# A decoder with a delta-rule layer: the inverses of its diagonal blocks in groups of four units, not eight

## The reference

```
q, k, v = silu(conv(x @ Wq)), silu(conv(x @ Wk)), silu(conv(x @ Wv))   # HK = 16 heads, q and k of 128, v of 256
q, k = l2norm(q), l2norm(k)
alpha, beta = sigmoid(x @ Wa), sigmoid(x @ Wb)
def step(state, (qt, kt, vt, at, bt)):
    state = state * at
    err = vt - einsum('bhkv,bhk->bhv', state, kt)
    state = state + bt * einsum('bhk,bhv->bhkv', kt, err)
    return state, einsum('bhkv,bhk->bhv', state, qt)
x = x + outs @ Wo
```

## Time and profile before

| what | value |
|---|---|
| median of 3 runs | 4774.38 us (4768.8 to 4774.94) |
| profiled execution | 4788.41 us, span 4786.6 us |
| busy in the span: PE, DVE, ACT, POOL | 82%, 58%, 34%, 28% |
| the delta layer | about 1518 to 3260 us |
| there: PE, DVE, ACT, POOL busy | 1645.6, 1354.4, 823.6, 889.1 us |
| mean granted clock of TensorE | 0.918 |

### The profile page before, as it was taken

How to read it: one execution, slowest core, us unless ns; L and a number is a source line. 1 busy time by engine, 2 the same in 40 slices (tenths; PEclk the granted TensorE clock), 3 DMA queues, 4 the chain that set the end, 5 groups by cost and what they waited for, 6 DMA issues and landing times. The chain is left out here.

```text
span 4786.6 us, 58979 instructions
## 1 busy us (share of the span) xinstructions
PE 3923.9 (82%) x18543; PEld 2940.0 (61%) x18543; DVE 2799.6 (58%) x7765; ACT 1611.4 (34%) x3960; POOL 1349.6 (28%) x2074
## 2 busy tenths in 40 slices
PE   6999976999997799999999999983999999960230
PEld 4666654555555578888888888872556565640230
DVE  4666654222222788888888888844666666653123
ACT  2444431111111455545455554521444444420000
POOL 0000000000000365455555455540111111116447
PEclk9999986999997999999999999996999999985665
DMA  1000000000000011111111111111000000011240
GB/s 65 0 0 0 0 8 24 12 12 23 12 12 18 20 37 23 41 38 24 36 23 40 35 29 36 24 18 51 1 0 0 0 0 0 0 64 58 60 143 13
DMA packets 198749, 119.39 MB, mean 25 GB/s; under 512 B 122312, under 2 KB 187654, under 8 KB 197520
## 3 DMA queue, kind: packets, MB, share of 16 engines
q1 hardware_dynamic: 181472, 102.85, 8.3%
q0 software_dynamic: 12288, 9.55, 0.7%
q10 hardware_dynamic: 4800, 4.72, 0.3%
HBM read 102.09 MB, written 38.93 MB: 29 GB/s over the span
## 5 line engine op out<-in xcount | busy, mean ns | idle before, releaser
L1630 DVE SCALAR_TENSOR_TENSOR dl_y<-ps,dl_taps,dl_y 128x255 f32<-128x255 f32 (+2 forms) x1536 | 653.0, 474 | 131.4 <-ACT dl_y L1526 127.3
L1361 PE MATMUL ps<-xnT,dl_wkqv 128*128 128x256 f32 x2048 | 543.4, 391 | 33.9 <-DVE dl_lp L1673 26.4
L923 PE MATMUL ps<-xnT,moe_wgu 128*112 x1024 | 447.3, 595 | 5.2 <-DVE moe_ex L963 5.2
L1361 PEld LDWEIGHTS ps<-xnT,dl_wkqv 128*128 128x128 f32 x2048 | 367.9, 193 | 84.0 <-issue 39.2
L923 PEld LDWEIGHTS ps<-xnT,moe_wgu 128*112 128x112 f32 x1024 | 181.9, 178 | 251.3 <-issue 249.3
L362 POOL TENSOR_TENSOR at_rs<-at_ss,mhalf 128x15 f32<-128x15 f32 x32 | 125.5, 3921 | 745.9 <-DVE at_ss L549 745.9
L183 POOL TENSOR_TENSOR ln_rstd<-ln_ve,mhalf 128x4 f32<-128x4 f32 x24 | 24.2, 1010 | 1084.0 <-DVE ln_ve L169 1084.0
L1284 POOL TENSOR_TENSOR dl_rn<-dl_n,mhalf 128x4 f32<-128x4 f32 x128 | 173.7, 1357 | 548.2 <-DVE dl_n L1646 548.2
L448 PE MATMUL ps<-at_shared,at_v 128*128 128x256 f32 (+2 forms) x1280 | 315.9, 380 | 4.6
L989 DVE TENSOR_TENSOR moe_hT<-moe_sg,ps 112x1024 f32<-112x1024 f32 x64 | 78.2, 1221 | 372.6 <-ACT moe_sg L947 372.6
L1526 ACT ACTIVATE dl_y<-ps,dl_taps 128x256 f32<-128x256 f32 x512 | 260.2, 560 | 95.4 <-PE ps L1361 95.4
(11 more groups left out here) (278 smaller groups left out, 8195.3 us busy)
## 6 DMA issues: line engine op xcount, KB each, us to landing
dl_grow<-decay_rows SPq DMA_DIRECT2D x128, 128.0 KB, 3.0
sp_wgu<-in_w1gu SPq DMA_DIRECT2D x12, 768.0 KB, 10.2
dl_wkqv<-in_w1kqv SPq DMA_DIRECT2D x16, 512.0 KB, 4.7
delta_diag<-dl_lp SPq DMA_DIRECT2D x512, 8.0 KB, 1.5
dl_diag<-delta_diag_tt SPq DMA_DIRECT2D x512, 8.0 KB, 1.7
moe_wgu<-in_w0gu SPq DMA_DIRECT2D x16, 448.0 KB, 3.7
slot_rows<-sp_zero SPq DMA_DIRECT2D x4, 1152.0 KB, 8.1
sp_wd<-in_w1d SPq DMA_DIRECT2D x12, 384.0 KB, 11.5
```

The lines of the kernel that those rows point to most:

```text
L923: last = nc.tensor.matmul(k.ps[h][0:IC, m, :], wgu[q][h][:, c, m * IC:(m + 1) * IC], k.xnT[:, c, ds(g * (GT * P), GT * P)], start=c == 0, ...
L1361: last = nc.tensor.matmul(bank(h, m // 2, (m % 2) * S, (m % 2 + 1) * S), wkqv[h][:, c, m * P:(m + 1) * P], k.xnT[:, c, u.seq * S:(u.seq + ...
L1630: last = nc.vector.scalar_tensor_tensor(y[h][:, m, back:S], bank(h, m // 2, (m % 2) * S, (m % 2 + 1) * S - back), taps[h][:, m, KC - 1 - b ...
```

## The change

Groups are of four units (GI = 4) on 32 partitions, and each is inverted in four stages, all four of which have two parts: `CUTS` has eight. LAG is 2 * GI + 2 = 10. `inv_a` has two buffers, so that its load waits for the end of the inversion before the last. A group is now named by the unit's number alone. On SP, `load_a` stands directly behind the last dump of its group, and `store_inverse` at the first grown unit of its group.

```diff
@@ -1020,16 +1020,19 @@
...
 
+GI = 4
+
+
 class Group:
...
 
-    def __init__(self, j, g):
-        self.j, self.g = j, g
-        self.parity = g % 2
-        self.real = not isinstance(j, int) or 0 <= 2 * j + g < HK * B // 8
+    def __init__(self, n):
+        self.g, self.inst = n // GI, n % GI
+        self.parity = self.g % 2
+        self.real = 0 <= n < HK * B
 
     def count(self, per, more=0):
-        return self.j * (2 * per) + (self.g * per + more)
+        return self.g * per + more
 
...
@@ -1078,15 +1081,13 @@
...
     Q32 = 32
-    GI = 8
     GP = GI * 8
...
     STEPS = 2 + 2 * (Q32 - 2)
-    CUTS = (1, 4, 6, 9, 11, 14, 16, 18, 20, 23, 25, 28, Q32 - 1)
-    CHUNKS = 6
-    LAG = 16
+    CUTS = (1, 5, 9, 13, 17, 20, 24, 28, Q32 - 1)
+    LAG = 2 * GI + 2
     scratch = nc.dram_tensor("decay_rows", (HK, T), F32, kind="Internal").ap()
...
@@ -1122,7 +1123,7 @@
...
 
-        inv_a = sb("inv_a", [GP, Q32, Q32])
+        inv_a = [sb(f"inv_a{i}", [GP, Q32, Q32]) for i in range(2)]
         inv_flat = sb("inv_u", [GP, Q32 * (Q32 + 1)])
...
@@ -1184,18 +1185,18 @@
...
 
-                def dump_diag(u, g, inst):
+                def dump_diag(u, g):
 
...
                         r = slice(b * Q32, (b + 1) * Q32)
-                        sp.dma_start(ldump[g.parity, o, inst].rearrange("b r c -> r b c"),
+                        sp.dma_start(ldump[g.parity, o, g.inst].rearrange("b r c -> r b c"),
                                      lp[u.h][r, u.seq, 0:2 * S].rearrange("p (b s) -> p b s", b=2)[:, :, r]).then_inc(dumped, 16)
...
                     sp.wait_ge(dumped, g.count(GI * 4 * 16, GI * 4 * 16))
-                    wait_past(sp, inv_done, g.count(1))
-                    sp.dma_start(inv_a[:, :, :], ldump[g.parity].rearrange("o i b r c -> (o i b) r c")).then_inc(a_loaded, 16)
+                    wait_past(sp, inv_done, g.count(1, -1))
+                    sp.dma_start(inv_a[g.parity][:, :, :], ldump[g.parity].rearrange("o i b r c -> (o i b) r c")).then_inc(a_loaded, 16)
 
...
@@ -1203,28 +1204,24 @@
...
 
-                def load_diag(u, g, inst):
+                def load_diag(u, g):
 
...
                         r = slice(b * Q32, (b + 1) * Q32)
-                        sp.dma_start(diag[u.h][r, :, r], ttdump[g.parity, o, inst].rearrange("b r c -> r b c"))\
+                        sp.dma_start(diag[u.h][r, :, r], ttdump[g.parity, o, g.inst].rearrange("b r c -> r b c"))\
                             .then_inc(diag_loaded[u.h], 16)
...
                         sp.dma_start(diag_t[u.h][o * HALF:o * HALF + Q32, :, o * Q32:(o + 1) * Q32],
-                                     tdump[g.parity, o, inst].rearrange("b r c -> r b c")).then_inc(diag_loaded[u.h], 16)
+                                     tdump[g.parity, o, g.inst].rearrange("b r c -> r b c")).then_inc(diag_loaded[u.h], 16)
 
                 def stage(j, s, project, prepared, turned, grown, given):
-                    first = Group(j, (s - 9) // 8)
-                    if s % 8 == 1 and first.real:
-                        load_a(first)
-                    if s % 8 == 7:
-                        done = Group(j, (s - 15) // 8)
-                        if done.real:
-                            store_inverse(done)
-                    ready = Unit(j, s - 15)
+                    n = 2 * B * j + s
+                    ready = Group(n - (LAG - 1))
                     if ready.real:
-                        load_diag(ready, Group(j, (s - 15) // 8), (s - 15) % 8)
+                        if ready.inst == 0:
+                            store_inverse(ready)
+                        load_diag(Unit(j, s - (LAG - 1)), ready)
                     ahead = Unit(j, s + 1)
...
@@ -1235,7 +1232,10 @@
...
                     if prepared is not None:
-                        dump_diag(prepared, Group(j, (s - 1) // 8), (s - 1) % 8)
+                        full = Group(n - 1)
+                        dump_diag(prepared, full)
+                        if full.inst == GI - 1:
+                            load_a(full)
 
...
@@ -1286,7 +1286,7 @@
...
                     wait_past(pool, inv_stored, g.count(32))
-                    nc.gpsimd.tensor_tensor(inv_u, inv_a[:, :, :], inv_mask[:, :, :], ALU.mult).then_inc(inv_step, 1)
+                    nc.gpsimd.tensor_tensor(inv_u, inv_a[g.parity][:, :, :], inv_mask[:, :, :], ALU.mult).then_inc(inv_step, 1)
                     pool.wait_ge(inv_step, g.count(STEPS, 1))
...
@@ -1297,7 +1297,7 @@
...
                     nc.gpsimd.tensor_tensor(tmp, inv_u[:, 0:i, i:i + 1].to_broadcast([GP, i, w]),
-                                            inv_a[:, i:i + 1, i + 1:Q32].to_broadcast([GP, i, w]), ALU.mult).then_inc(inv_step, 1)
+                                            inv_a[g.parity][:, i:i + 1, i + 1:Q32].to_broadcast([GP, i, w]), ALU.mult).then_inc(inv_step, 1)
                     pool.wait_ge(inv_step, g.count(STEPS, 2 * i + 1))
...
@@ -1312,20 +1312,20 @@
...
                         eliminate(g, i)
-                    if part == 2 * CHUNKS - 1:
+                    if part == 2 * GI - 1:
                         end_inverse(g)
...
                 def stage(j, s, project, prepared, turned, grown, given):
-                    g, part = Group(j, (s - 9) // 8), (s - 1) % 8
-                    inverting = g.real and part < CHUNKS
+                    g = Group(2 * B * j + s - GI - 1)
+                    inverting = g.real
                     if prepared is not None:
...
                     if inverting:
-                        invert_part(g, 2 * part)
+                        invert_part(g, 2 * g.inst)
                     if prepared is not None:
...
                     if inverting:
-                        invert_part(g, 2 * part + 1)
+                        invert_part(g, 2 * g.inst + 1)
 
...
@@ -1418,7 +1418,7 @@
...
 
-                    pe.wait_ge(v_scaled[h], min(u.count(1, B), B * HK // 2) if u.fixed else u.count(1, B))
+                    pe.wait_ge(v_scaled[h], min(u.count(1, LAG // 2), B * HK // 2))
                     for blk in range(2):
...
@@ -2212,7 +2212,7 @@
...
     r, q = np.arange(32)[:, None], np.arange(32)[None, :]
-    c["c_invmask"] = np.broadcast_to(np.where(q > r, -1.0, 0.0).astype(np.float32), (64, 32, 32))
+    c["c_invmask"] = np.broadcast_to(np.where(q > r, -1.0, 0.0).astype(np.float32), (32, 32, 32))
     return c
...
```

## The result

The changed kernel takes 4833.31 us (median of 4 runs, 4826.41 to 4840.09) where the kernel before took 4774.66 in as many runs beside it: a ratio of 1.0122, 95% interval 1.0100 to 1.0144, so 58.7 us slower. The forecast was 4861 (+87), with a range of 4795 to 4920. Its direction and its mechanism held; it was too high by 28 us. In the experiments further down one run of e3 stood apart, with 5242 us where its other five took 4750 to 4755; the ratio is of those five.

The account below looks back on a forecast made before the run. PE with DVE paced the kernel before; POOL would bound the changed one. First to last pow +111.8 us, drain -25.2, together +86.6: profiled 4788.41 becomes 4875.0, less 14.0 to the median, 4861 us, range 4795 to 4920.

Parts of the forecast that it names:

- The drain: The layer's end after the last pow: 25.2 us less, 24.0 of it from fewer units behind the last inversion.
- POOL's instructions cost the same on 32 partitions: POOL's inversion on 32 partitions takes the same 38.91 us per group as on 64, run 32 times instead of 16.
- The rival "faster": POOL's operations cost half on 32 partitions; late gap 13.0 us, total about 4724 us; chance 0.06.
- The three gaps without a load: The three intervals between pows in a group that hold no load: 35.71 us of POOL work plus 1.8 of stalls.
- The pow: POOL's power of each unit's lengths (L1284), starting each stage: hardly waits for DVE, 1.02 us rather than 1.40.
- The first gap: Interval between pows at a group's start: 10.1 us until load and stores land, 5.72 for the first part, 15.8 together.
- The sum: First to last pow: 30.3 us of fill plus 31 groups of 53.3 give 1682.6, +111.8; with the drain +86.6.
- POOL becomes the bound, by 2 us a group: POOL paces the stages: 53.3 us per group of four, where the other engines could do it in 51.4.
- The waits: DVE waits 150 us or more for the pow; POOL about 90% busy, PE 93%; 32 L1289 waits of about 4 us.
- What was costed at nothing: Second inv_a, head weights, load_diag behind the stores, and PE's clock in the fill: each taken to add no time.
- The gentle case: Everything hides but the load, no stalls: 50.7 us a group, 4780 us (4776 to 4825); chance 0.18.
- the heavy case: Load and stores in series (12.24 us), or full lock between POOL and DVE: 4926 to 4932 us; chance 0.08 (above 4915).

Follow-up runs that it names:

- e3: Changed kernel with two buffers for inv_u, each group's inversion begun one stage later and LAG 12: 0.9953 of the kernel before, 4751.23 us.
- e5: Changed kernel with DVE's first L1640 of a stage reading its second operand from PSUM: 1.0053 of the kernel before.
- e11: Changed kernel with 11 eliminations left out of the middle of each group's inversion, first and last part whole: 1.0008 of the kernel before.
- e8: Changed kernel, LAG 10 kept, with the pow ahead of the inversion's start in a group's first stage: 1.0007 of the kernel before.
- e10: Changed kernel, LAG 10, with the pow first, two buffers for inv_u and two POOL copies per stage removed: 0.9952 of the kernel before.
- e6: Kernel before (groups of eight, LAG 16) with each of a group's 60 eliminating instructions issued twice: 1.0376 of the kernel before.
- e9: Kernel before (groups of eight, LAG 16) with the pow ahead of the inversion in a group's first stage: 0.9968 of the kernel before.
- e7: e3 with POOL relieved of two copies per stage, ACT using three activations instead of two: 0.9877 of the kernel before.
- e4: Changed kernel with 13 of each group's 30 eliminations left out, the wait kept: 1.0082 of the kernel before.

## Why the prediction was right, and where its sizes were off

**The drain.** Forecast: 25.2 us less. From the last pow to the end of the last add it was 116.0 us and is 3322.88 + 0.88 - 3233.53 = 90.2: 25.8 less. Right, though divided a little differently: behind the last inversion it is 25.2 less and not 24.0, while its start comes 12.55 us after the pow, hardly sooner than the 12.7 of before, where 10 to 12 was forecast.

```profile
L1284 POOL TENSOR_TENSOR dl_rn<-dl_n,mhalf x128: 1014/1023/1462, 1567.9 to 3233.5; 128x4 f32<-128x4 f32 x128
```
```profile
3322.88 0.88 DVE L1710 SCALAR_TENSOR_TENSOR x<-ps,dl_rq,x 128x256 f32<-128x256 f32 x2 [4.18 <-PE ps L1471]
```

**POOL's instructions cost the same on 32 partitions.** Right: 662 against 669 ns. The rival "faster" fell with it.

**The three gaps without a load.** Forecast 35.71 + 1.8 = 37.5; measured 12.58 + 12.70 + 12.16 = 37.44, and without the first of two stalls 35.66 (e5). The sum is right, and that is in part luck: the stalls cost 2.7 us a group (0.9 a gap, from two collisions of mostly 0.3 to 0.6 each) and POOL's own work 34.7, so the two terms were each off by 1 us, in opposite directions.

**The pow.** Forecast: it hardly waits for DVE, and takes 1.02 instead of 1.40. It does in 111 of 128 cases (before in 15). The other 17 are pows on time, as at 2971.69 in the earlier trace rows, which start some 0.1 us behind the end of L1646, when DVE's second L1640 has just begun, and take 1.39 to 1.46.

**The first gap: the mis-sized term.** "The gap is then 10.1 + 5.72 = 15.8 us" was 14.90 in the median and 15.24 in the mean. The part after the start was right (5.71). The 10.1 was read from loads and stores of twice the bytes (3.0 to 3.4 us); the halved load lands 2.2 us after its issue (2.0 to 2.9) and the stores 2.1 in the median, so the start comes at 9.17. Against this stands something that was not foreseen: in 12 of 31 groups the gap is 15.6 to 16.4. In ten of them SP is late: in four one store took 1.29 to 1.60 us to issue, in six the four dumps took 2.37 to 2.74 instead of 1.72. In the other two (and one of the six) the pow at the head of the gap was on time, took 1.41 to 1.43, and the dump began 4.01 us behind its start instead of 3.25. One of each of the first two kinds:

```profile
2236.75 1.60 SPq L1203 DMA_DIRECT2D delta_diag_tt<-dl_inv_u  x1
...
2240.71 2.35 POOL L1289 TENSOR_TENSOR dl_inv_u<-dl_inv_a,dl_inv_mask 32x1024 f32<-32x1024 f32 x1 [4.00 <-DMA delta_diag_t<-dl_inv_t]
...
2288.80 2.37 SPq L1193 DMA_DIRECT2D delta_diag<-dl_lp  x4
```

The Trainium skill ("SBUF — State Buffer", The DMA setup-cost knee) gives a transfer some 2 us plus its bytes over 436 GB/s, the rate of all 16 ports; an estimate by that line is 2.3 us for 128 KB and 2.6 for 256 KB. The 128 KB loads of after agree, with 2.2 in the median; the 256 KB loads of before took 3.2 to 3.6, longer than by that line, and there the measurement decides.

**The sum.** A group was forecast at 53.3 and takes 52.68: 31 x 0.62 = 19 us less. The three gaps of the fill took 32.7, not 30.3: 2.4 more, which isn't the change's (see below). So from first to last pow it is 1665.7, not 1682.6 (+94.9 rather than +111.8). The layer's set-up, not in the sum, is 3.5 us shorter; it is 50.9 to 53.6 us in all the kernels with groups of four and 54.5 to 54.9 in the three with groups of eight. Whether the mask of half the bytes does it isn't shown. 94.9 - 25.8 - 3.5 = 65.6, the layer's +65.7. From the forecast's +86.6 this is 21 us off. The other 7 of the 28 lie between these two executions and the medians (+65.7 and +58.7): the profiled execution of before was 13.8 us above its median, which about its slower layers behind account for (14.8), that of after was 4.0 above its own, and its layer began 2.0 earlier.

**"POOL becomes the bound, by 2 us a group."** Right in kind. The other engines' 51.4 is what e11 gives, 51.41. POOL leads them by 52.68 - 51.41 = 1.3, not 1.9. The three short gaps differ by the 1.9 forecast (37.44 against 35.55 in e11); the forecast had the first gap at 15.8 on both sides, and it is 15.24 behind a late pow and 15.85 behind one on time. What the sum didn't say is how the 3.0 us above the old 49.69 divide: 1.7 is the late gap that now comes twice as often and stays when POOL has less to do (e11), and 1.3 is that POOL can't catch up behind it. These aren't two prices to be paid apart: taking the wait off the pow's way gives back 2.9 us a group in e3 and 2.0 in e8, with all of POOL's work in place.

**The waits.** L1655 waits 125.0 us in 86 places, where 150 or more over a hundred were forecast; PE's share is 95.3% and not 93; POOL's 85.5% and not 90. A shorter first gap goes the way of the first two, but it would raise POOL's share. That was forecast too high because POOL is not counted busy in the short pauses between its dependent eliminations, which the 38.91 us contain: by the page they are 75.2 + 58.3 us, 4.2 a group, or 8% of it (the idle time, the last number of each line):

```profile
L1302 POOL TENSOR_TENSOR dl_inv_u<-dl_inv_u,dl_inv_tmp 32x30 f32<-32x30 f32 (+14 forms) x960 | 532.2, 554 | 75.2
L1299 POOL TENSOR_TENSOR dl_inv_tmp<-dl_inv_u,dl_inv_a 32x30 f32<-32x30 f32 (+14 forms) x960 | 486.2, 506 | 58.3
```

L1289: 32 waits of about 4 us were forecast; to 3200 us there are 31, of 3.3 us. That the stores end last there, and not the load, was right.

**What was costed at nothing.** PE doesn't wait for `load_diag` here, as said; with the inverses only a part of a stage later it does (e8, e10), so this cover was thin. The clock in the fill fell to 0.89 in the first stretch where it had been 0.98, and the three gaps there grew by 2.4 us in all; later it is 0.99 as before. This came with the execution and not with the change: e6 and e9, with groups of eight and the same code up to there, have 32.7 us in these three gaps too, at a clock of 0.90. The first stretch in the kernel before, and then in e9:

```profile
1568.00:1650.00 82.00, 63.95 (x287) 49.42 (x287) 67.21 (x171) 41.91 (x88) 20.85 (x40) 0.98 0.07 16
```
```profile
1568.00:1650.00 82.00, 67.98 (x279) 52.27 (x280) 63.18 (x162) 41.29 (x87) 20.86 (x40) 0.90 0.06 15
```

**The other rivals.** The gentle case had its first gap at 9.26 + 5.72 = 14.98, which is what the undisturbed groups show (14.90), but no stalls in the other three, and these are 1.7 us a group above its 35.71. Of the heavy case, load and stores in series would start the inversion 12.24 us after the pow, and it starts at 9.17; the full 0.69 at each of two collisions would make the three gaps 35.71 + 4.1 = 39.8, and they are 37.44: there are two collisions a gap, at mostly 0.3 to 0.6 us each.

## What to carry to other kernels

Work that is sized by the elements in a partition doubles when a group is halved, and a wait at a group's start comes twice as often: price both, and look at what stands behind the waiting instruction on its engine. Before the last stage of a lag is taken out, compare the way of the data that it covers (here 9.2 us from pow to start) with the work that stands ahead of the wait (6.3 us). Twelve stages (e3, e7) beat both sixteen and ten here, as far as it was tried: e7's relief of POOL was not run with groups of eight, and without it e3's 0.9953 is barely below the 0.9968 of the old kernel with the pow first (e9), with intervals that overlap. And when work is taken away without gain, look at each gap before the theory is dropped: in e4 a copy had only slid onto another engine's instructions.

## What the runs showed of the hardware

- A tiny DVE instruction was held for as long as a long POOL instruction ran: 128x2 products took 1.84 us beside a POOL copy of 1.95, and 2.13 beside a multiplication of 2.35, and ended within 0.03 us of it. The Trainium skill ("SBUF — State Buffer", Who interferes with whom) says that the loser blocks for the whole instruction. These cases agree in full; where POOL's elimination met DVE's product of 0.68 us it lost mostly 0.3 to 0.6 (0.40 in the median of 209 meetings in after).
- A DVE product with one operand in PSUM held nothing up: the same POOL instruction took 0.56 us beside it and 1.14 beside one with both in SBUF (e5). The Trainium skill ("SBUF — State Buffer", SBUF: two separate sides) lets only those DVE operations compete that have two inputs in SBUF or run in a 2-port performance mode. e5 agrees as to the inputs; no run here shows the modes.
- A DMA issue on SP that takes 0.42 us took 1.29 to 1.60 in 4 of 32 cases at one line. No run tells why.
- POOL's elimination takes 662 ns on 32 partitions of 240 elements and 669 on 64.
- Left open: why the layers behind take some 1513 us in nine profiles and some 1525 in five, and why SP is sometimes slow to issue.
